# A 64-expert transformer layer: each expert's weights in one transfer, in six joint buffers

## The chip, the core and the metric

The kernel runs on one core of a Trainium2 chip. The core has TensorE (PE) for matrix products, VectorE (DVE), ScalarE (ACT), GpSimd (POOL) and SyncE (SP), which here only issues DMAs, and 16 DMA engines that move data between device memory and SBUF. The engines run side by side and are ordered by semaphores alone. The metric is the device time of one execution in microseconds (us); lower is better.

## The reference, cut to what matters

```python
# x: 4096 tokens of 512; attention with a decaying running sum, then a mixture of 64 experts
x = layernorm(x + attention(x, w_qkv, w_out, decay))

scores = softmax(xf @ gate_w.T)                 # 4096 x 64
topk_w, topk_idx = top_k(scores, 6)
# each expert has up to 128 slots (CAP): buf_tok (64, 128) names tokens, buf_w their weights
gx = xp[buf_tok]                                # 64 x 128 x 512, the gathered rows
g, u = split(einsum("ech,ehi->eci", gx, gate_up_proj))   # gate_up_proj: 64 x 512 x 384
hid = silu(g) * u                               # 64 x 128 x 192
eo = einsum("eci,eih->ech", hid, down_proj) * buf_w      # down_proj: 64 x 192 x 512
routed = zeros.at[buf_tok].add(eo)
shared = (silu(xf @ sg.T) * (xf @ su.T)) @ sd.T          # one shared expert of width 384
x = layernorm(x + routed + shared)
```

All is float32. The kernel reaches that precision by splitting operands into a rounded part (hi, float32r) and a rest (lo), and adding three products.

## The kernel before

The work runs in three stages. First the attention, eight blocks (`NB`) of 512 tokens (`BT`), with the routing of each tile of 128 tokens behind it; it ends at about 460 us. Then the experts, one after another (`NE` = 64), with work units of the shared expert between them. Last the remaining shared units, which take the second normalisation with them.

The order of each engine is written by hand, one function per engine inside `build` (`sync`, `scalar`, `vector`, `gpsimd`, `tensor`). Nothing is scheduled by a tool.

An expert e takes these steps. POOL gathers its 128 rows from `x1_rows` into `xg` (`gather`, 2304 bytes a row, six buffers `NXG`, issued four experts ahead, `AHEAD`). SP loads its gate-up weights (`load_gate_up`, L466, 128 partitions x 6144 bytes) and its down weights (`load_down`, L471, 128 x 3072 bytes). ACT rounds the gate-up weights into `wgu_hi` (`split_expert`, L904), DVE writes the rest `wgu_lo` over the weights in the buffer (L1454). PE turns the rows (`turn_rows`, L1956), multiplies them (L1717), turns the hidden values (L1999), and multiplies them with the down weights (`down`, also L1717, since every product goes through the helper `chain`). ACT scales the output rows by the token weight into `eo` (`scale_rows`, L918), and POOL adds them to the rows in device memory with an indirect DMA (`add_rows`, L1657).

PE's iteration e is: product of expert e, `down(e - 1)`, the shared units of this iteration if it has any (`fills_of`), `turn_rows(e + 2)`, the turn of the hidden values. ACT and DVE convert the weights of e + 2 in iteration e.

There are five gate-up buffers (`NG`) and five down buffers (`ND`). SP's loop for the experts, behind the loads of experts 0 to 4, is:

```python
for e in range(NE):
    if e + NG < NE:
        load_gate_up(e + NG)      # waits until gu_mm >= e + 1: the product of expert e is done
    if e and e - 1 + ND < NE:
        load_down(e - 1 + ND)     # waits until eo_mm >= e: down(e - 1) is done
```

POOL's loop issues `add_rows(e - 2)` and then `gather(e + 4)`. An add waits for its output rows and, since two adds to one of the two sum arrays must not overlap, for the landing of the add two experts before it (`rows_added[e % 2]`). The gather is queued behind it.

The input block of the shared expert (`x1t_stage`, 1 MB) is loaded from ACT's queue (`load_x1t`, L760) once for each eight units.

Three DMA queues appear in the profile: q1 is that of SP, q10 that of ACT, q0 that of POOL.

Of the kernel before, what the change touches and what calls it, by code (L numbers as in the profile page):

```python
# [7 lines left out]
F32 = mybir.dt.float32  # L8
F32R = mybir.dt.float32r
# [6 lines left out]
P = 128  # L16
# [24 lines left out]
def three(a_hi, a_lo, b_hi, b_lo):  # L41

    return [(a_hi, b_hi), (a_hi, b_lo), (a_lo, b_hi)]


def build(nc, x, x_t, w_qkv, w_out, decay_param, gate_t, w_gu, w_down, sg_t, su_t, sd_t, out):
    T, D = x.shape
    E, _, _, GU = w_gu.shape
    I = GU // 2
    SI = sg_t.shape[1]  # L50
    BT = 512
    NB = T // BT
    NJ = BT // P
# [1 line left out]
    KC = D // P  # L55
    SC = SI // P
    IB = I - P
    DH = D // 2
    DN = D + DH
    KS = KC - 0  # L60
    SLOTS = E * CAP
    HW = D // HEADS
    TAIL = 4
    EARLY = NB - TAIL
    SET = 1
    NG, ND, NXG, AHEAD = 5, 5, 6, 4
    STEPS = NB * KC
    UNITS = 2 * SC + NJ // 2

# [9 lines left out]
    both = Map(nc, start, end)  # L79
# [7 lines left out]
    FRING = 8  # L87
    fin_sum, fin_mean, fin_square, fin_rstd, fin_shift = [both.place(f"fin_{s}", [P, FRING])
                                                          for s in ("sum", "mean", "square", "rstd", "shift")]
    wgu_at = [both.at + 4 * i * KC * GU for i in range(2)]  # L90
    wgu_buf = [both.place(f"wgu{i}", [P, KC, GU]) for i in range(2)]
    wdn_buf = [both.place(f"wdn{i}", [P, DN]) for i in range(2)]

    att = Map(nc, both.at, end)
    wqkv_hi = att.place("wqkv_hi", [P, 3 * KC, KC, P], F32R)
# [77 lines left out]
    xs_at = lo_at + KC * chunk  # L173
# [22 lines left out]

    late = Map(nc, projected_end, kept_from)

    wgu_at += [late.at + 4 * i * KC * GU for i in range(NG - 3)]
    wgu_buf += [late.place(f"wgu{i}", [P, KC, GU]) for i in range(2, NG - 1)]  # L200

    wdn_buf += [late.place(f"wdn{i}", [P, DN]) for i in range(2, ND - 1)]
    assert late.at >= projected_end + 8 * 4 * BT

    shared_rows = [late.place(f"shared_rows{b}", [P, NJ, D]) for b in range(EARLY - SET)]
# [2 lines left out]
    xgt_hi = [late.place(f"xgt_hi{i}", [P, KS, P], F32R) for i in range(2)]  # L208
    xgt_lo = [late.place(f"xgt_lo{i}", [P, KS, P], F32R) for i in range(2)]
    eo = [Map(nc, x_at + 2 * half - 4 * D, x_at + 2 * half).place("eo0", [P, D]),  # L210
          Map(nc, xs_at + 4 * BT, xs_at + 8 * BT).place("eo1", [P, D]),
          Map(nc, x_at + 4 * half - 4 * D, x_at + 4 * half).place("eo2", [P, D])]
    silu_e = late.place("silu_e", [P, I])
    hid_e = [late.place(f"hid_e{i}", [P, 2 * P]) for i in range(2)]
    hid_et = [late.place(f"hid_et{i}", [P, P]) for i in range(2)]
    het_hi = [late.place(f"het_hi{i}", [P, P], F32R) for i in range(2)]
    het_lo = [late.place(f"het_lo{i}", [P, P], F32R) for i in range(2)]

# [1 line left out]
    late.end = end  # L220
    wgu_hi = [late.place(f"wgu_hi{i}", [P, KS, GU], F32R) for i in range(2)]
    wdn_mix = [late.place(f"wdn_mix{i}", [P, D], F32R) for i in range(2)]
    xg += [late.place(f"xg{i}", [P, D + E]) for i in range(NXG - 2, NXG)]
    eo.append(late.place("eo3", [P, D]))
    wgu_at.append(late.at)
    wgu_buf.append(late.place(f"wgu{NG - 1}", [P, KC, GU]))
    wdn_buf.append(late.place(f"wdn{ND - 1}", [P, DN]))
    wgu_lo = [Map(nc, at, at + 4 * KC * GU).place(f"wgu_lo{i}", [P, KS, GU], F32R) for i, at in enumerate(wgu_at)]


    fin_map = Map(nc, both.at - 2 * 4 * (KC * GU + DN), both.at)
# [10 lines left out]
    NE, NEO = E, len(eo)  # L242
# [48 lines left out]
    for e in range(NE):  # L291
        n = 0
# [37 lines left out]
    with ExitStack() as ctx:  # L330
# [3 lines left out]
        def sems(name, n):  # L334
            return [sem(f"{name}{i}") for i in range(n)]
# [5 lines left out]
        xg_ps, gu_ps, ht_ps, eo_ps = banks[3], banks[4:6], banks[6], banks[7]  # L341
        hot_ps, last_ps = banks[6], banks[6]

        def rows_bank(i):
# [11 lines left out]

        SCALED, ROUNDED = 1, 2
        TABLE_READ, TABLE_TURNED, TABLE_JOINED = 1, 2, 3
        gu_in, dn_in, xg_in, rows_added = sems("gu_in", NG), sems("dn_in", ND), sems("xg_in", NXG), sems("rows_added", 2)
        zeroed, shared_out, x1t_in = sem("zeroed"), sems("shared_out", SET), sem("x1t_in")  # L360
        fin_in, odd_in, fin_out = sems("fin_in", NFA), sems("odd_in", NFB), sems("fin_out", NFA)

# [14 lines left out]
        xgt_hi_done, wgu_hi_done, silu_e_done, het_hi_done, eo_done = (  # L377
            sem("xgt_hi_done"), sem("wgu_hi_done"), sem("silu_e_done"), sem("het_hi_done"), sem("eo_done"))
# [51 lines left out]
        def _(sp):  # L430
# [29 lines left out]
                    sp.wait_ge(x1_added, i - 1)  # L460
                sp.dma_start(xres[i % 2][:, :], x[i * P:(i + 1) * P, :]).then_inc(xres_in[i % 2], 16)

            def load_gate_up(e):
                if e >= NG:
                    sp.wait_ge(gu_mm, e - NG + 1)
                sp.dma_start(wgu_buf[e % NG][:, :, :], w_gu[e]).then_inc(gu_in[e % NG], 16)  # L466

            def load_down(e):
                if e >= ND:
                    sp.wait_ge(eo_mm, e - ND + 1)  # L470
                sp.dma_start(wdn_buf[e % ND][:, :], w_down[e]).then_inc(dn_in[e % ND], 16)  # L471

            def clear_sums(b):
                dst = acc_dram[1][b * BT:(b + 1) * BT, :].rearrange("(p r) (n w) -> p (r n) w", p=P, w=P)
# [87 lines left out]
            sp.wait_ge(num_done, STEPS)  # L562
            sp.wait_ge(qk_done, STEPS)
            sp.wait_ge(state_done, STEPS)
            for e in range(2, NG - 1):
                load_gate_up(e)
            load_down(2)
            store_turned(LAST - 3)
            store_x1(LAST - 3)
            store_score(LAST - 4)  # L570
            store_x1(LAST - 2)
            sp.wait_ge(heads_mm, NB)
            load_down(3)
            sp.wait_ge(shared_split, 2)
            for e in range(2):
                load_gate_up(e)
            store_turned(LAST - 2)
            store_score(LAST - 3)
            store_score(LAST - 2)
# [3 lines left out]
            load_xres(NB - 1, 3)  # L583
            store_score(LAST - 1)
            sp.wait_ge(shared_split, 2 + SC)
            for e in range(2):
                load_down(e)
            for i in range(LAST, NT):
                store_x1(i)
                store_turned(i)  # L590
# [9 lines left out]
                sp.wait_ge(x1_out[lane], 16 * NT // NJ)  # L600
                sp.wait_ge(acc_out[lane], 16 * NT // NJ)
            sp.wait_ge(table_done, TABLE_JOINED)
            load_gate_up(NG - 1)
            load_down(ND - 1)
            for e in range(NE):
                if e + NG < NE:
                    load_gate_up(e + NG)
                if e and e - 1 + ND < NE:
                    load_down(e - 1 + ND)

            def load_first(m):
                b = block_order[m]
# [38 lines left out]
        def _(act):  # L651
# [246 lines left out]
                act.copy(xgt_hi[e % 2][:, :, :], xg_ps[:, :].rearrange("p (k s) -> p k s", k=KC)).then_inc(xgt_hi_done, 1)  # L898

            def split_expert(e):  # L900
                act.wait_ge(gu_in[e % NG], 16 * (e // NG + 1))
                if e >= 2:
                    act.wait_ge(gu_mm, e - 1)
                act.copy(wgu_hi[e % 2][:, :, :], wgu_buf[e % NG][:, 0:KS, :]).then_inc(wgu_hi_done, 1)  # L904

            def split_down_of(e):
                act.wait_ge(dn_in[e % ND], 16 * (e // ND + 1))
                if e >= 2:
                    act.wait_ge(eo_mm, e - 1)
                w, mix = wdn_buf[e % ND], wdn_mix[e % 2]  # L910
                act.copy(mix[0:IB, 0:DH], w[0:IB, D:DN])
                act.copy(mix[IB:P, DH:D], w[IB:P, D:DN]).then_inc(wdn_hi_done, 1)

# [101 lines left out]
        def _(dve):  # L1015
# [435 lines left out]

            def split_expert(e):
                dve.wait_ge(wgu_hi_done, e + 1)
                dve.tensor_tensor(wgu_lo[e % NG][:, :, :], wgu_buf[e % NG][:, 0:KS, :], wgu_hi[e % 2][:, :, :].bitcast(F32),  # L1454
                                  ALU.subtract).then_inc(wgu_lo_done, 1)

            def split_down_of(e):
                dve.wait_ge(wdn_hi_done, e + 1)
                w, mix = wdn_buf[e % ND], wdn_mix[e % 2]
                dve.tensor_tensor(mix[IB:P, 0:DH], w[0:IB, D:DN], mix[0:IB, 0:DH].bitcast(F32), ALU.subtract)  # L1460
                dve.tensor_tensor(mix[0:IB, DH:D], w[IB:P, D:DN], mix[IB:P, DH:D].bitcast(F32), ALU.subtract).then_inc(wdn_lo_done, 1)

# [251 lines left out]
        def _(pe):  # L1714
            def chain(out_ap, products, first=True, final=True):
                for i, (a, b) in enumerate(products):
                    mm = pe.matmul(out_ap, a, b, start=first and i == 0, stop=final and i == len(products) - 1)  # L1717
                return mm
# [240 lines left out]
            def down(e):  # L1959
                pe.wait_ge(het_lo_done, e + 1)  # L1960
                pe.wait_ge(wdn_lo_done, e + 1)
                if e:
                    pe.wait_ge(eo_done, e)
                products = [(part[e % 2][:, :], wdn_mix[e % 2][:, :]) for part in (het_hi, het_lo)]
                chain(eo_ps[:, :], products, final=False)
                chain(eo_ps[:, :], [(hid_et[e % 2][:, :], wdn_buf[e % ND][:, 0:D])], first=False).then_inc(eo_mm, 1)

            for _ in range(BEFORE_EXPERTS[0]):
                unit()
# [10 lines left out]
            for e in range(NE):  # L1980
                pe.wait_ge(xgt_lo_done, e + 1)
                if e >= 2:
                    pe.wait_ge(hid_e_done, e - 1)
                pe.wait_ge(wgu_lo_done, e + 1)
                products = []
                for k in range(KS):
                    products += three(xgt_hi[e % 2][:, k, :], xgt_lo[e % 2][:, k, :], wgu_hi[e % 2][:, k, :], wgu_lo[e % NG][:, k, :])
                chain(gu_ps[e % 2][:, 0:GU], products).then_inc(gu_mm, 1)
                if e:
                    down(e - 1)  # L1990
                for _ in range(fills_of[e]):
                    unit()
                if e + 2 < NE:
                    turn_rows(e + 2)
                pe.wait_ge(hid_e_done, e + 1)
                if e:
                    pe.wait_ge(het_lo_done, e)
                for h in range(2):
                    mm = pe.transpose(ht_ps[:, h * P:(h + 1) * P], hid_e[e % 2][:, h * P:(h + 1) * P], ident[:, :])  # L1999
                mm.then_inc(ht_mm, 1)  # L2000
# [37 lines left out]
```

## Time and profile before

| | us |
|---|---|
| median of 3 runs | 913.0 |
| the three runs | 909.56, 913.0, 913.59 |
| the profiled execution | 914.21 |
| its span, first to last instruction | 911.6 |
| expert stage, about | 480 to 808 |

The median is the time to compare with. The profiled execution is a single one; its rows sum up to its own time, 2.6 us of which lie outside the span. Busy time of PE is modelled from the starts of its pipelined products. An engine's idle time is shown in brackets, with what ended it behind the arrow.

### The profile page before, as it was taken

Reading aid. Unit: us, or ns where it says so; the run is one execution under the profiler, and the core shown is the slowest. Engines: PE = TensorE matmul, PEld = TensorE weight load, DVE = VectorE, ACT = ScalarE, POOL = GpSimd, SP = SyncE. Lnnn points to the kernel's source line nnn. Section 1 sums busy time; section 2 is a strip of 40 time slices with the busy share of each in tenths; the row PEclk is TensorE's granted clock in tenths of the full one; section 3 lists DMA queues with packets and bytes.
Section 4 is the critical chain, followed back from the end, with each engine's and each line's share of the span. In section 5 each row is a group of like instructions: output and inputs, shape, how many; then the busy total and the mean of one; then the engine's idle time right before and its main releaser. Section 6 shows DMA issues by size and latency. Waiting matters only on the chain. (4 is left out here: it accounts for less than half of the span.)

```text
span 911.6 us, 15597 instructions
## 1 busy us (share of the span) xinstructions
PE 892.3 (98%) x4635; PEld 727.5 (80%) x4635; DVE 718.9 (79%) x1422; ACT 549.0 (60%) x1208; POOL 488.1 (54%) x540
## 2 busy tenths in 40 slices
PE   8999999999999999999999999999999999999997
PEld 7788888888888788777888788888788888877875
DVE  6997887979788897898857788887778887736776
ACT  5532535434353443544558878888778888736785
POOL 2002366565566656577434656766566666533665
PEclk9999999999999999999999999999999999999999
DMA  6343563536263333439567999999999999959963
GB/s 211 97 161 116 145 140 103 133 89 173 74 188 96 123 103 116 144 101 336 181 224 238 333 360 354 357 337 323 348 342 347 336 346 324 298 106 391 378 249 129
DMA packets 111634, 203.95 MB, mean 224 GB/s; under 512 B 18496, under 2 KB 50240, under 8 KB 110528
## 3 DMA queue, kind: packets, MB, share of 16 engines
q1 hardware_dynamic: 91024, 159.87, 51.2%
q0 software_dynamic: 19520, 35.75, 16.3%
q10 hardware_dynamic: 1008, 7.34, 2.1%
q8 instruction: 38, 0.62, 0.3%
q14 instruction: 44, 0.36, 0.1%
HBM read 143.03 MB, written 59.88 MB: 223 GB/s over the span
## 5 line engine op out<-in xcount | busy, mean ns | idle before, releaser
L1612 POOL DMA_INDIRECT slot_table<-tokens,slot_of x162 | 180.3, 1113 | 86.9 <-issue 50.4
L1657 POOL DMA_INDIRECT acc_rows<-eo,table_sb x64 | 137.1, 2142 | 119.8 <-DMA acc_rows<-eo,table_sb 61.8
L1717 PE MATMUL bank<-x_hi,wqkv_hi 128*128 128x512 f32 x384 | 152.1, 396 | 1.6 <-DVE wqkv_lo L1022 1.6
L1717 PE MATMUL bank<-x_hi,wqkv_lo 128*128 128x512 f32 x384 | 150.1, 391 | 0.0
L1717 PE MATMUL bank<-x_lo,wqkv_hi 128*128 128x512 f32 x384 | 150.1, 391 | 0.0
L1454 DVE TENSOR_TENSOR wgu_lo<-wgu,wgu_hi 128x1536 fp32r<-128x1536 f32 x64 | 112.1, 1752 | 2.6 <-ACT wgu_hi L904 1.9
L904 ACT CAST wgu_hi<-wgu 128x1536 fp32r<-128x1536 f32 x64 | 94.2, 1473 | 1.6 <-issue 0.4
L1646 POOL DMA_INDIRECT xg<-x_rows,table_sb x64 | 73.4, 1147 | 36.3 <-issue 19.0
L1717 PE MATMUL bank<-wgu_hi,xgt_hi 128*128 128x384 f32 x256 | 91.9, 359 | 0.0
L674 ACT ACTIVATE e<-bank 128x512 f32<-128x512 f32 x64 | 38.0, 594 | 81.4 <-PE bank L1717 81.4
L1717 PEld LDWEIGHTS bank<-x_hi,wqkv_hi 128*128 128x128 f32 x384 | 72.2, 188 | 17.5 <-DVE wqkv_lo L1022 1.8
L1717 PE MATMUL bank<-wgu_lo,xgt_hi 128*128 128x384 f32 x256 | 86.1, 336 | 0.0
L1717 PE MATMUL bank<-wgu_hi,xgt_lo 128*128 128x384 f32 x256 | 86.0, 336 | 0.0
L1717 PEld LDWEIGHTS bank<-x_hi,wqkv_lo 128*128 128x128 f32 x384 | 72.0, 188 | 15.5
L1717 PEld LDWEIGHTS bank<-x_lo,wqkv_hi 128*128 128x128 f32 x384 | 72.2, 188 | 15.1
L1596 POOL TENSOR_SCALAR rstd<-mv 128x1 f32<-128x1 f32 x32 | 9.8, 307 | 123.1 <-DVE mv L1049 121.9
L1717 PE MATMUL bank<-wdn,hid_et 128*128 128x512 f32 x128 | 65.3, 591 | 0.0
L1956 PEld LDWEIGHTS bank<-ident,xg 128*128 128x128 f32 x256 | 30.4, 141 | 33.8 <-issue 25.2
L1467 DVE TENSOR_TENSOR het_lo<-bank,het_hi 128x128 fp32r<-128x128 f32 x64 | 18.6, 291 | 45.3 <-ACT het_hi L957 45.0
L1717 PE MATMUL bank<-wout_hi,att_hi 128*128 128x512 f32 x128 | 52.3, 408 | 1.1 <-issue 0.6
L1717 PE MATMUL bank<-wout_lo,att_hi 128*128 128x512 f32 x128 | 50.2, 393 | 0.0
L1717 PE MATMUL bank<-wout_hi,att_lo 128*128 128x512 f32 x128 | 50.2, 392 | 0.0
(198 smaller groups left out, 2300.0 us busy)
## 6 DMA issues: line engine op xcount, KB each, us to landing
wgu<-w_gu SPq DMA_DIRECT2D x64, 768.0 KB, 7.3
wdn<-w_down SPq DMA_DIRECT2D x64, 384.0 KB, 8.0
xres<-x SPq DMA_DIRECT2D x32, 256.0 KB, 3.4
x_turned<-x1t SPq DMA_DIRECT2D x32, 256.0 KB, 2.9
x_rows<-x SPq DMA_DIRECT2D x32, 256.0 KB, 3.1
acc_rows<-x SPq DMA_DIRECT2D x32, 256.0 KB, 2.8
fin<-acc_rows SPq DMA_DIRECT2D x8, 1024.0 KB, 11.9
odd<-acc_rows SPq DMA_DIRECT2D x8, 1024.0 KB, 13.9
```

The lines of the kernel that those rows point to most:

```text
L674: act.activation(e_sb[q][:, :], ps[:, :], ACT.Exp)
L904: act.copy(wgu_hi[e % 2][:, :, :], wgu_buf[e % NG][:, 0:KS, :]).then_inc(wgu_hi_done, 1)
L1454: dve.tensor_tensor(wgu_lo[e % NG][:, :, :], wgu_buf[e % NG][:, 0:KS, :], wgu_hi[e % 2][:, :, :].bitcast(F32), ALU.subtract).then_inc(wgu_ ...
L1467: dve.tensor_tensor(het_lo[e % 2][:, :], ht_ps[:, P:2 * P], het_hi[e % 2][:, :].bitcast(F32), ALU.subtract).then_inc(het_lo_done, 1)
L1596: pool.tensor_scalar(rstd[i][:, :], mv[i][:, 1:2], EPS_NORM, None, ALU.add).then_inc(norm_done, 1)
L1612: pool.indirect_dma_start(table_dram, bass.IndirectOffsetOnAxis(slot_of[:, i, k:k + 1], 0), tokens[:, i:i + 1], None, bounds_check=SLOTS - ...
L1646: pool.indirect_dma_start(xg[e % NXG][:, :], None, x1_dram, bass.IndirectOffsetOnAxis(table_sb[:, e:e + 1], 0), bounds_check=T - 1, oob_is ...
L1657: pool.indirect_dma_start(acc_dram[e % 2], bass.IndirectOffsetOnAxis(table_sb[:, e:e + 1], 0), eo[eo_slot[e]][:, :], None, bounds_check=T ...
L1717: mm = pe.matmul(out_ap, a, b, start=first and i == 0, stop=final and i == len(products) - 1)
L1956: mm = pe.transpose(xg_ps[:, k * P:(k + 1) * P], xg[e % NXG][:, k * P:(k + 1) * P], ident[:, :])
```

## The change

The host places an expert's down weights behind its gate-up weights, so that both are one row of 9216 bytes for each partition (`w_expert`). One DMA (`load_expert`) fills one of six joint buffers (`NW` = 6), with one semaphore (`we_in`). The buffer is free when `down` of its former expert is done (`eo_mm`); gate-up and down weights are views of it. The first six experts are loaded ahead: 2, 3, 0 and 1 during the last attention block, 4 and 5 when the routing table is ready. To make room, `silu_e` and `hid_et` lie where the `tanh_s` tile of shared block 0 stood.

```diff
-    NG, ND, NXG, AHEAD = 5, 5, 6, 4
+    NW, NXG, AHEAD = 6, 6, 4
...
-    silu_e = late.place("silu_e", [P, I])
+    small = Map(nc, xs_at, xs_at + 4 * BT)
+    silu_e = small.place("silu_e", [P, I])
     hid_e = [late.place(f"hid_e{i}", [P, 2 * P]) for i in range(2)]
-    hid_et = [late.place(f"hid_et{i}", [P, P]) for i in range(2)]
+    hid_et = [small.place(f"hid_et{i}", [P, P]) for i in range(2)]
...
+    we_at += [late.at + 4 * i * WE for i in range(NW - 4)]
+    we_buf += [late.place(f"we{i}", [P, WE]) for i in range(4, NW)]
+    wgu_buf = [we[:, 0:KC * GU].rearrange("p (k n) -> p k n", k=KC) for we in we_buf]
+    wdn_buf = [we[:, KC * GU:WE] for we in we_buf]
...
-            def load_gate_up(e):
-                if e >= NG:
-                    sp.wait_ge(gu_mm, e - NG + 1)
-                sp.dma_start(wgu_buf[e % NG][:, :, :], w_gu[e]).then_inc(gu_in[e % NG], 16)
-
-            def load_down(e):
-                if e >= ND:
-                    sp.wait_ge(eo_mm, e - ND + 1)
-                sp.dma_start(wdn_buf[e % ND][:, :], w_down[e]).then_inc(dn_in[e % ND], 16)
+            def load_expert(e):
+                if e >= NW:
+                    sp.wait_ge(eo_mm, e - NW + 1)
+                sp.dma_start(we_buf[e % NW][:, :], w_expert[e]).then_inc(we_in[e % NW], 16)
...
-            for e in range(2, NG - 1):
-                load_gate_up(e)
-            load_down(2)
+            load_expert(2)
...
             sp.wait_ge(heads_mm, NB)
-            load_down(3)
+            load_expert(3)
             sp.wait_ge(shared_split, 2)
-            for e in range(2):
-                load_gate_up(e)
+            load_expert(0)
...
             sp.wait_ge(shared_split, 2 + SC)
-            for e in range(2):
-                load_down(e)
+            load_expert(1)
...
-            load_gate_up(NG - 1)
-            load_down(ND - 1)
-            for e in range(NE):
-                if e + NG < NE:
-                    load_gate_up(e + NG)
-                if e and e - 1 + ND < NE:
-                    load_down(e - 1 + ND)
+            for e in range(4, NE):
+                load_expert(e)
...
             def split_expert(e):
-                act.wait_ge(gu_in[e % NG], 16 * (e // NG + 1))
+                act.wait_ge(we_in[e % NW], 16 * (e // NW + 1))
...
             def split_down_of(e):
-                act.wait_ge(dn_in[e % ND], 16 * (e // ND + 1))
+                act.wait_ge(we_in[e % NW], 16 * (e // NW + 1))
```

SP's order moves; the other engines keep theirs. These rows are of SP, at the start of the expert stage, before the change (the number in a name tells the buffer; `gu_mm` and `eo_mm` count products and down products done):

```order
234 L471 DMA wdn_211<-w_down 128x768
235 L466 DMA wgu_70<-w_gu 128x1536 [waits gu_mm]
236 L466 DMA wgu_71<-w_gu 128x1536 [waits gu_mm]
237 L471 DMA wdn_72<-w_down 128x768 [waits eo_mm]
238 L466 DMA wgu_176<-w_gu 128x1536 [waits gu_mm]
239 L471 DMA wdn_73<-w_down 128x768 [waits eo_mm]
```

The same place of SP with the change, from the load of expert 3's successor, expert 4 (buffer 206):

```order
228 L475 DMA acc_rows<-shared_rows_176 128x4x512 [waits rows_copied]
229 L466 DMA we_206<-w_expert 128x2304 [waits x1_out2,acc_out1,acc_out2,x1_out1,x1_out3,acc_out0,acc_out3,x1_out0,table_done,x1t_out1,x1t_out0]
230 L466 DMA we_207<-w_expert 128x2304
231 L466 DMA we_70<-w_expert 128x2304 [waits eo_mm]
232 L466 DMA we_71<-w_expert 128x2304 [waits eo_mm]
```

Expert 5's weights (row 230) now follow those of expert 4 without a wait, and every later expert is one load that waits for a down product.

During the last attention block SP's queue had this before the change:

```order
192 L466 DMA wgu_176<-w_gu 128x1536 [waits state_done,qk_done,num_done]
193 L466 DMA wgu_177<-w_gu 128x1536
194 L471 DMA wdn_178<-w_down 128x768
195 L484 DMA x_turned<-x1t_143 512x1x128 [waits x1t_done]
...
201 L471 DMA wdn_179<-w_down 128x768 [waits heads_mm]
202 L466 DMA wgu_70<-w_gu 128x1536 [waits shared_split]
203 L466 DMA wgu_71<-w_gu 128x1536
...
213 L471 DMA wdn_72<-w_down 128x768 [waits shared_split]
214 L471 DMA wdn_73<-w_down 128x768
```

And with the change:

```order
192 L466 DMA we_174<-w_expert 128x2304 [waits state_done,qk_done,num_done]
193 L479 DMA x_turned<-x1t_141 512x1x128 [waits x1t_done]
...
199 L466 DMA we_175<-w_expert 128x2304 [waits heads_mm]
200 L466 DMA we_70<-w_expert 128x2304 [waits shared_split]
...
210 L466 DMA we_71<-w_expert 128x2304 [waits shared_split]
```

Eight loads became four, at the places of the later half of each pair; expert 1 (`we_71`) moved behind eight stores and loads, to where its down half was.

## Rows read from the trace of the kernel before

In a row of waits stand the waiting engine and line, what ended the wait, total us, times and the longest. A row of a timeline has start and duration in us, engine, line, operation and how many. A row of a DMA queue has packets, MB and the share of 16 engines' time; a row of an issue has how many, KB, and the middle time from issue to landing in us.

**Rows 1.** The page: busy us and share of PE; DMA share in 40 slices.

```profile
PE 892.3 (98%) x4635; PEld 727.5 (80%) x4635; DVE 718.9 (79%) x1422; ACT 549.0 (60%) x1208; POOL 488.1 (54%) x540
DMA  6343563536263333439567999999999999959963
```

**Rows 2.** Busy us by stretch: PE, PEld, DVE, ACT, POOL; granted clock, DMA share, GB/s.

```profile
480.00:808.00 328.00, 323.04 (x1653) 267.17 (x1652) 257.79 (x466) 263.94 (x540) 200.14 (x121) 0.99 0.99 324
656.80:660.00 3.20, 3.20 (x13) 3.20 (x14) 1.22 (x2) 1.61 (x5) 0.32 (x1) 0.50 1.06 362
```

**Rows 3.** Waits in 486 to 808 us.

```profile
POOL acc_rows L1657 <- DMA acc_rows<-eo,table_sb: 61.8, 30, 3.6
...
PEld bank L1956 <- DMA xg<-x_rows,table_sb: 5.6, 4, 2.9
...
PE bank L1956 <- DMA xg<-x_rows,table_sb: 2.5, 2, 2.0
```

**Rows 4.** Timeline of PE: the longest wait for gathered rows.

```profile
656.73 1.12 PE L1956 MATMUL bank<-ident,xg 128*128 128x128 f32 x4 [2.04 <-DMA xg<-x_rows,table_sb]
```

**Rows 5.** Timelines of POOL and PE, and between them this gather's time to landing.

```profile
548.37 1.06 POOL L1646 DMA_INDIRECT xg<-x_rows,table_sb  x1 [0.31 <-issue]
...
xg<-x_rows,table_sb POOLq DMA_INDIRECT x1, 7.7
...
556.79 0.60 PE L1956 MATMUL bank<-ident,xg 128*128 128x128 f32 x4
```

**Rows 6.** Timeline of SP's issues in 600 to 606 us, and gate-up landings.

```profile
601.04 0.33 SPq L466 DMA_DIRECT2D wgu<-w_gu  x1
602.37 0.33 SPq L471 DMA_DIRECT2D wdn<-w_down  x1
605.31 0.33 SPq L466 DMA_DIRECT2D wgu<-w_gu  x1
...
DMA to landing us min/median/max: 5.0/7.5/11.4
```

**Rows 7.** DMA queues and issues of POOL in 486 to 800 us.

```profile
q1 hardware_dynamic: 16835, 68.74, 57.5%
q0 software_dynamic: 13280, 32.84, 41.7%
q10 hardware_dynamic: 432, 3.15, 2.4%
...
acc_rows<-eo,table_sb POOLq DMA_INDIRECT x61, 9.1
xg<-x_rows,table_sb POOLq DMA_INDIRECT x58, 7.8
```

**Rows 8.** DMA queues in 651 to 654 us, while x1t_stage is loaded.

```profile
q10 hardware_dynamic: 87, 0.71, 56.0%
q0 software_dynamic: 87, 0.28, 25.9%
q1 hardware_dynamic: 68, 0.22, 18.9%
```

**Rows 9.** DMA queues in 657 to 663 us.

```profile
q1 hardware_dynamic: 335, 1.35, 56.9%
q0 software_dynamic: 305, 0.82, 48.9%
```

**Rows 10.** The first expert's gather: POOL's issue, its landing, PE's transposes.

```profile
462.51 1.06 POOL L1646 DMA_INDIRECT xg<-x_rows,table_sb  x1 [16.97 <-DVE table_sb L1183]
...
xg<-x_rows,table_sb POOLq DMA_INDIRECT x1, 8.2
...
471.89 0.60 PE L1956 MATMUL bank<-ident,xg 128*128 128x128 f32 x4
```

More of the change, by code:

```diff
@@ L43, in three, with build @@
     return [(a_hi, b_hi), (a_hi, b_lo), (a_lo, b_hi)]
-def build(nc, x, x_t, w_qkv, w_out, decay_param, gate_t, w_gu, w_down, sg_t, su_t, sd_t, out):
+def build(nc, x, x_t, w_qkv, w_out, decay_param, gate_t, w_expert, sg_t, su_t, sd_t, out):
     T, D = x.shape
-    E, _, _, GU = w_gu.shape
+    E, SI = w_expert.shape[0], sg_t.shape[1]
+    GU = (w_expert.shape[2] - D - D // 2) // (D // P)
     I = GU // 2
-    SI = sg_t.shape[1]
     BT = 512
@@ L59, in build @@
     DN = D + DH
+    WE = KC * GU + DN
     KS = KC - 0
@@ L89, in build @@
                                                           for s in ("sum", "mean", "square", "rstd", "shift")]
-    wgu_at = [both.at + 4 * i * KC * GU for i in range(2)]
-    wgu_buf = [both.place(f"wgu{i}", [P, KC, GU]) for i in range(2)]
-    wdn_buf = [both.place(f"wdn{i}", [P, DN]) for i in range(2)]
+    we_at = [both.at + 4 * i * WE for i in range(2)]
+    we_buf = [both.place(f"we{i}", [P, WE]) for i in range(2)]
     att = Map(nc, both.at, end)
@@ L197, in build @@
     late = Map(nc, projected_end, kept_from)
-    wgu_at += [late.at + 4 * i * KC * GU for i in range(NG - 3)]
-    wgu_buf += [late.place(f"wgu{i}", [P, KC, GU]) for i in range(2, NG - 1)]
-    wdn_buf += [late.place(f"wdn{i}", [P, DN]) for i in range(2, ND - 1)]
+    we_at += [late.at + 4 * i * WE for i in range(2)]
+    we_buf += [late.place(f"we{i}", [P, WE]) for i in range(2, 4)]
     assert late.at >= projected_end + 8 * 4 * BT
@@ L224, in build @@
     eo.append(late.place("eo3", [P, D]))
[L225 to L228, printed above, removed]
+    we_at += [late.at + 4 * i * WE for i in range(NW - 4)]
+    we_buf += [late.place(f"we{i}", [P, WE]) for i in range(4, NW)]
+    wgu_buf = [we[:, 0:KC * GU].rearrange("p (k n) -> p k n", k=KC) for we in we_buf]
+    wdn_buf = [we[:, KC * GU:WE] for we in we_buf]
+    wgu_lo = [Map(nc, at, at + 4 * KC * GU).place(f"wgu_lo{i}", [P, KS, GU], F32R) for i, at in enumerate(we_at)]
     fin_map = Map(nc, both.at - 2 * 4 * (KC * GU + DN), both.at)
@@ L358, in build @@
         TABLE_READ, TABLE_TURNED, TABLE_JOINED = 1, 2, 3
-        gu_in, dn_in, xg_in, rows_added = sems("gu_in", NG), sems("dn_in", ND), sems("xg_in", NXG), sems("rows_added", 2)
+        we_in, xg_in, rows_added = sems("we_in", NW), sems("xg_in", NXG), sems("rows_added", 2)
         zeroed, shared_out, x1t_in = sem("zeroed"), sems("shared_out", SET), sem("x1t_in")
@@ L900, in split_expert @@
             def split_expert(e):
-                act.wait_ge(gu_in[e % NG], 16 * (e // NG + 1))
+                act.wait_ge(we_in[e % NW], 16 * (e // NW + 1))
                 if e >= 2:
                     act.wait_ge(gu_mm, e - 1)
-                act.copy(wgu_hi[e % 2][:, :, :], wgu_buf[e % NG][:, 0:KS, :]).then_inc(wgu_hi_done, 1)
+                act.copy(wgu_hi[e % 2][:, :, :], wgu_buf[e % NW][:, 0:KS, :]).then_inc(wgu_hi_done, 1)
             def split_down_of(e):
-                act.wait_ge(dn_in[e % ND], 16 * (e // ND + 1))
+                act.wait_ge(we_in[e % NW], 16 * (e // NW + 1))
                 if e >= 2:
                     act.wait_ge(eo_mm, e - 1)
-                w, mix = wdn_buf[e % ND], wdn_mix[e % 2]
+                w, mix = wdn_buf[e % NW], wdn_mix[e % 2]
                 act.copy(mix[0:IB, 0:DH], w[0:IB, D:DN])
@@ L1453, in split_expert @@
                 dve.wait_ge(wgu_hi_done, e + 1)
-                dve.tensor_tensor(wgu_lo[e % NG][:, :, :], wgu_buf[e % NG][:, 0:KS, :], wgu_hi[e % 2][:, :, :].bitcast(F32),
+                dve.tensor_tensor(wgu_lo[e % NW][:, :, :], wgu_buf[e % NW][:, 0:KS, :], wgu_hi[e % 2][:, :, :].bitcast(F32),
                                   ALU.subtract).then_inc(wgu_lo_done, 1)
@@ L1458, in split_down_of @@
                 dve.wait_ge(wdn_hi_done, e + 1)
-                w, mix = wdn_buf[e % ND], wdn_mix[e % 2]
+                w, mix = wdn_buf[e % NW], wdn_mix[e % 2]
                 dve.tensor_tensor(mix[IB:P, 0:DH], w[0:IB, D:DN], mix[0:IB, 0:DH].bitcast(F32), ALU.subtract)
@@ L1965, in down @@
                 chain(eo_ps[:, :], products, final=False)
-                chain(eo_ps[:, :], [(hid_et[e % 2][:, :], wdn_buf[e % ND][:, 0:D])], first=False).then_inc(eo_mm, 1)
+                chain(eo_ps[:, :], [(hid_et[e % 2][:, :], wdn_buf[e % NW][:, 0:D])], first=False).then_inc(eo_mm, 1)
             for _ in range(BEFORE_EXPERTS[0]):
@@ L1986, in _ @@
                 for k in range(KS):
-                    products += three(xgt_hi[e % 2][:, k, :], xgt_lo[e % 2][:, k, :], wgu_hi[e % 2][:, k, :], wgu_lo[e % NG][:, k, :])
+                    products += three(xgt_hi[e % 2][:, k, :], xgt_lo[e % 2][:, k, :], wgu_hi[e % 2][:, k, :], wgu_lo[e % NW][:, k, :])
                 chain(gu_ps[e % 2][:, 0:GU], products).then_inc(gu_mm, 1)
@@ L2026 @@
         "decay_param": decay, "gate_t": a["L0_ffn_gate_w"].T,
-        "w_gu": gu, "w_down": down,
+        "w_expert": np.concatenate([gu.reshape(experts, P, -1), down], axis=2),
         "sg_t": a["L0_ffn_shared_gate_w"].T, "su_t": a["L0_ffn_shared_up_w"].T, "sd_t": a["L0_ffn_shared_down_w"].T,
```

## Prediction

> **What bounds the kernel now.** I read the page first, then the idle times by what ended them, then the DMA queues of the expert stage. The page says that PE is busy for 98% of the span [rows 1], so the end is set by TensorE and only its gaps can be won. In the expert stage, 480 to 808 us, it is idle for 328.0 - 323.0 = 5.0 us, while the 16 DMA engines are occupied 0.99 of the time [rows 2]. So two things are full at once: PE does about 328 / 64 = 5.13 us of work per expert, and the DMA engines carry about as much as they can in that time. The expert stage contains everything that the change touches.
>
> The reader should next look at who makes PE wait there. PE waits for no weights. It waits for the gathered token rows (xg): 2.5 us on the matmuls in 2 cases, 5.6 us on the weight loads in 4 [rows 3]. The longest case is at 656.73 us: 2.04 us idle before the transposes of xg [rows 4]. Right behind it the granted clock is 0.50, which is the 1.2 GHz level, for the 3.2 us of 656.8 to 660 [rows 2], where PE does half as much: another 1.6 us. One late gather thus cost about 3.6 us. The gathers are thin elsewhere too. The one issued at 548.37 took 7.7 us and landed at 556.07, and its transposes started at 556.79, a margin of 0.7 us [rows 5]. POOL, which issues them, itself waits 61.8 us in 30 cases for an earlier add of output rows to land before it may issue the next add, and each gather stands behind such an add in its queue [rows 3].
>
> The weights have room. A gate-up load goes out when the product of expert e-5 ends and is converted during iteration e-2, three iterations later. The shortest iterations last 605.31 - 601.04 = 4.27 us, so the lead is at least 12.8 us, against landings of 7.5 us in the middle and 11.4 us at worst [rows 6].
>
> **The change part by part.**
>
> *Issues.* 128 weight transfers become 64. SP only waits in the loop and nothing but the next weight load is queued behind it, so the 64 issues less are worth nothing on any path.
>
> *Placement of the load.* Both orders show it: the joint load waits for eo_mm where gate-up waited for gu_mm. It is issued where the down load stands now, 602.37 - 601.04 = 1.33 us after the gate-up load [rows 6]. For gate-up that is 1.33 us later, for down one iteration earlier. The lead becomes 12.8 - 1.3 = 11.5 us. The joint landing I take as 7.5 us plus 384 KB at the stage's 324 GB/s [rows 2], 1.2 us, so 8.7 us: 2.8 us of margin, and zero on PE. If the worst landing (11.4 + 1.2 = 12.6) met the shortest three iterations, PE would lose 1.1 us; that is the bound upward, and there is none below zero, since PE never waited for weights.
>
> *DMA work.* In 486 to 800 us the weight queue q1 holds 57.5% of 314 us, the gather-and-add queue q0 41.7% [rows 7]; the 58 gathers issued there count the experts. Per expert and DMA engine q1 has 3.11 us in 16835 / 16 / 58 = 18.1 packets, 0.172 us each; q0 has 2.26 us in 14.3 packets, 0.158 us each. A row of gate-up (6 KB) and one of down (3 KB) become one packet of 9 KB; with the completion entries q1 has 9 packets per expert instead of 18. What that saves lies between nothing and the price per byte of the 8 KB packets of q10: 56.0% of 16 x 3 us for 0.71 MB, 37.9 us per MB, against 56.9% of 16 x 6 us for 1.35 MB, 40.5 us per MB, for q1 now [rows 8, 9]. That is at most 6%, 0.2 us of 3.11 per expert; 9 KB is nearest to 8 KB, so I take 0.2. It is DMA time, not PE time: it only shows where a gather was late.
>
> *Turns between the queues.* This is the term that decides. In 657 to 663 us, both queues full, q1 sends 335 packets and q0 305 [rows 9]; in 651 to 654 us, with a third queue loading the shared block's input, q10, q0 and q1 send 87, 87 and 68 packets, but 0.71, 0.28 and 0.22 MB [rows 8]. The engines share by packets, not by bytes. The Trainium skill, page DMA: Bandwidth & Descriptors, section Queues, rings and completion order, says that an engine goes round the queues that have work, packet by packet; the trace agrees by those counts. So a q0 packet today waits for a q1 packet of 0.172 us; the 14.3 packets of one expert need 14.3 x (0.158 + 0.172) = 4.72 us when q1 always has work. Afterwards they meet all nine weight packets, 2.26 + (3.11 - 0.2) = 5.17 us. q0 gets through later by 0.45 us per expert. Since the gather stands behind an add that waits for an earlier add, it can be hit twice: 0.9 us, bounds 0 (if the turns fall between bursts) and 1.5. The weights land sooner in exchange, where nobody waits.
>
> At 0.9 us the two stalls that PE has deepen by 1.8 us together, and margins like the 0.7 us of [rows 5] turn into 0.2 us each; I allow three: 0.6 us. Sum: +2.4 us.
>
> *Start of the stage.* Expert 5's load now goes out right behind expert 4's, together with the first gathers, instead of after the first product. The first gather is issued at 462.51 and lands 8.2 us later; its transposes start at 471.89, 1.2 us of margin [rows 10]. Its four packets per engine would each wait for 0.32 us instead of 0.17, 0.6 us in all, so the margin covers it: zero. If the gather had to wait for all of the extra 2.9 us of weights, 1.7 us would be lost. Expert 1 is loaded where its down half stood, among the last blocks of the attention and well ahead of the gathers: zero. The six buffers and the moved small ones wait for nothing new, because the tanh tile is last used in shared block 0, which ends before the experts: zero.
>
> **Sum.** The profiled execution took 914.2 us, 1.2 above the median of 913.0. 914.2 + 2.4 = 916.6, less 1.2: about **915.5 us**.
>
> **The rivals.**
>
> *Add chain (slower).* If q0 takes longer per expert than PE, POOL falls behind and every gather is late. The point is 5.13 us per expert. By the above q0 needs 5.17 us, and the three block loads of q10 add 2.4% of 314 us, 0.13 us per expert [rows 7]: 5.30. Over 58 experts 0.17 x 58 = 10 us, less the 2 us of margin that gathers have on the way: +8 us, 921 us. For it: POOL already waits for adds in 30 of 61 cases. Against it: the experts that carry a shared unit take longer, and q0 catches up there, and the shares of [rows 8, 9] add up to over 100%, so packets overlap a little.
>
> *Relief (faster).* Less DMA work and one burst instead of two leave the engines a pause, the gather at 656.73 lands in time, and 2.0 + 1.6 us go, with the 0.4 us of the other stall: 914.2 - 4.1 - 1.2 = 909 us. More is not to be had, since PE waits for nothing else of the change. For it: the fastest of the three runs, 909.56 us, lies just there, as if one run had had no such stall. Against it: q0's turn gets worse while the total falls by under 4%. The rules for kernel authors on the same page of the Trainium skill ask for DMAs of 1 MiB and more, and by its fit (2.0 us plus bytes at 436 GB/s) two loads of 3.8 and 2.9 us would become one of 4.7, an estimate of 2.0 us per expert; these loads overlap with others, so no PE time follows, and it speaks for this rival alone.
>
> *No effect.* The hardware cuts a 9 KB row into packets of the old size. Then turns and prices stay, and only the 1.33 us later issue is left: 913 us.
>
> **How the numbers follow.** Chances: the forecast 0.40 (913 to 917.5), the add chain 0.30, relief 0.22, no effect 0.08. About 0.5%, 4.6 us, is what a measurement of this kernel can tell from no change. Slower by more: the add chain without its mild end, 0.28, and 0.04 from the forecast's upper bound. Faster by more would need less than 908.4 us, 0.10 of the relief case. The range 909 to 922 takes in the relief value and the add chain's 921; outside lie its worse forms.
>
> **What would show it.** Packets of 9 KB in q1, nine per engine and expert. The middle landing of gathers above 7.8 us and of adds above 9.1 us, the weights' landing little above 7.5 us; PE's wait for xg above 2.5 us, always in front of the transposes. More of POOL's wait on adds than 61.8 us would point to the chain. Gathers landing sooner than now would prove the turn term wrong, and PE waiting for the weight conversion would prove the margin wrong.

## The result, and the profile after

The changed kernel takes 936.82 us at the median (934.69 to 937.7), against 913.05 us before: ratio 1.0259, 95% interval 1.0238 to 1.0279. It is 24 us slower where 2.5 us were forecast, and lies outside the range. The profiled execution took 936.49 us with a span of 934.7 us, so the rows below account for 23 us of span. A few executions of the later sets ran far slower than the rest (984 to 2593 us) and are left out of every ratio.

The stretches of the expert stage answer to [rows 2]; the columns are those of that group.

```profile
480.00:830.00 350.00, 325.43 (x1653) 265.96 (x1651) 257.96 (x466) 265.75 (x542) 189.16 (x120) 1.00 0.96 301
809.10:812.50 3.40, 3.40 (x12) 3.40 (x12) 2.56 (x3) 1.61 (x5) 2.15 (x2) 0.51 0.84 202
```

The stage now lasts until about 830 us instead of 808. PE's idle time in it is 350.0 - 325.4 = 24.6 us, where it was 5.0 us, and PE is busy 2.4 us longer for the same 1653 matmuls: 22 of the 23 us of span are here. DVE and ACT are busy as long as before, and the DMA engines move less per second (301 GB/s against 324). There is one clock drop again, to 0.51 in 809.1 to 812.5 us. As before, it stands right behind one of the longest waits for gathered rows, the one that ends at 808.22.

Who made PE wait is told by the waits of 480 to 830 us, against [rows 3]:

```profile
POOL acc_rows L1643 <- DMA acc_rows<-eo,table_sb: 88.3, 36, 4.5
...
PEld bank L1942 <- DMA xg<-x_rows,table_sb: 42.4, 28, 4.2
...
PE bank L1942 <- DMA xg<-x_rows,table_sb: 23.1, 20, 3.4
```

The gathered rows it is, 23.1 us in 20 cases instead of 2.5 us in 2. No row of waits names the weights. The longest cases in PE's timeline, against [rows 4]:

```profile
523.99 0.66 PE L1942 MATMUL bank<-ident,xg 128*128 128x128 f32 x4 [1.65 <-DMA xg<-x_rows,table_sb]
...
663.93 0.55 PE L1942 MATMUL bank<-ident,xg 128*128 128x128 f32 x3 [3.36 <-DMA xg<-x_rows,table_sb]
...
808.22 0.66 PE L1942 MATMUL bank<-ident,xg 128*128 128x128 f32 x4 [3.00 <-DMA xg<-x_rows,table_sb]
```

The DMA queues and issues of 486 to 820 us, against [rows 7]:

```profile
q1 hardware_dynamic: 8352, 68.42, 55.9%
q0 software_dynamic: 13244, 32.80, 40.9%
q10 hardware_dynamic: 432, 3.15, 2.3%
...
we<-w_expert SPq DMA_DIRECT2D x58, 1152.0 KB, 8.8
...
acc_rows<-eo,table_sb POOLq DMA_INDIRECT x60, 10.2
xg<-x_rows,table_sb POOLq DMA_INDIRECT x58, 9.6
```

q1 has half the packets for the same bytes: 8352 / 16 / 58 = 9 per engine and expert. A gather takes 9.6 us to land at the median instead of 7.8, an add 10.2 instead of 9.1. Both queues in 640 to 655 us, around the longest wait, first before the change and then with it:

```profile
q1 hardware_dynamic: 645, 2.67, 45.7%
q0 software_dynamic: 660, 1.66, 42.7%
...
q1 hardware_dynamic: 394, 3.32, 62.7%
q0 software_dynamic: 532, 1.32, 36.2%
```

Over the 16 engines q0 gets 532 / 15 = 35 packets per us here, where it got 660 / 15 = 44, with q10 at work beside it. This is a bad stretch and not the rule: in 664 to 670 us it gets 282 / 6 = 47, and over the whole window it falls only from 13280 / 314 = 42 to 13244 / 334 = 40. Six of these 15 us, 645 to 651, show the turns at their clearest. q1 sends 166 packets and q0 142, nearly one for one as in [rows 9], and that is 24 per us for q0. One gather issued in this stretch takes 14.7 us to land.

### The profile page after: what moved, and what is told of

It is laid out like the page before. It is cut to its first block and busy times, and to the rows that moved or that the text cites. A ratio compares the mean times of both kernels' runs of the same rounds, so it can differ in the third digit from the quotient of the medians.

```text
span 934.7 us, 15533 instructions
## 1 busy us (share of the span) xinstructions
PE 895.7 (96%) x4635; PEld 727.4 (78%) x4635; DVE 719.0 (77%) x1422; ACT 549.9 (59%) x1208; POOL 476.9 (51%) x540
## 5 line engine op out<-in xcount | busy, mean ns | idle before, releaser
L1643 POOL DMA_INDIRECT acc_rows<-eo,table_sb x64 | 125.0, 1953 | 152.9 <-DMA acc_rows<-eo,table_sb 88.3
L1440 DVE TENSOR_TENSOR wgu_lo<-we,wgu_hi 128x1536 fp32r<-128x1536 f32 x64 | 112.0, 1752 | 2.6 <-ACT wgu_hi L890 1.9
L890 ACT CAST wgu_hi<-we 128x1536 fp32r<-128x1536 f32 x64 | 94.2, 1473 | 1.6 <-issue 0.4
L1703 PE MATMUL bank<-we,hid_et 128*128 128x512 f32 x128 | 65.3, 592 | 0.0
L1942 PE MATMUL bank<-ident,xg 128*128 128x128 f32 x256 | 39.8, 278 | 23.6 <-DMA xg<-x_rows,table_sb 23.1
## 6 DMA issues: line engine op xcount, KB each, us to landing
odd<-acc_rows SPq DMA_DIRECT2D x8, 1024.0 KB, 13.9
```

The costliest lines, as they stand in the source:

```text
L890: act.copy(wgu_hi[e % 2][:, :, :], wgu_buf[e % NW][:, 0:KS, :]).then_inc(wgu_hi_done, 1)
L1440: dve.tensor_tensor(wgu_lo[e % NW][:, :, :], wgu_buf[e % NW][:, 0:KS, :], wgu_hi[e % 2][:, :, :].bitcast(F32), ALU.subtract).then_inc(wgu_ ...
L1643: pool.indirect_dma_start(acc_dram[e % 2], bass.IndirectOffsetOnAxis(table_sb[:, e:e + 1], 0), eo[eo_slot[e]][:, :], None, bounds_check=T ...
L1942: mm = pe.transpose(xg_ps[:, k * P:(k + 1) * P], xg[e % NXG][:, k * P:(k + 1) * P], ident[:, :])
```

## The experiments

Two theories stood against each other. **Turns:** the DMA engines serve the queues packet by packet, so larger weight packets make every packet of a gather or an add wait longer. **Burst:** what harms is that 1.15 MB are issued in one piece, later, and on top of the gather. A third, **chain**, puts the loss down to POOL's order, in which the gather stands behind an add that waits for an earlier add. All ratios below are to the kernel before, run on the same chip. They are not the quotients of the two medians and differ from them by up to 0.2%. The runs came in three sets on three chips, and each trace is of a single execution.

### The joint load with 3 KB packets

Only the layout in device memory changes; the DMA, its place and its wait stay.

```diff
-sp.dma_start(we_buf[e % NW][:, :], w_expert[e])
+sp.dma_start(we_buf[e % NW][:, :].rearrange("p (c n) -> p c n", c=3), w_expert[e].rearrange("c p n -> p c n"))
```

> The changed kernel with one edit: in device memory an expert's weights lie in three pieces of 3072 bytes for each partition, so the joint load stays one DMA at the same place with the same wait, but moves 3 KB packets instead of 9 KB ones. Theory turns (DMA engines serve the queues packet by packet, so a gather or add packet waits for a whole weight packet): a gather or add packet waits for 0.12 us of weights instead of 0.36, gathers land in 7.8 us or less at the median, PE's wait for gathered rows falls from 23 us to under 3, 909 to 914 us. Theory burst (the load of 1.15 MB in one piece, 1.3 us later and on top of the gather, is what delays it): nothing moves, 935 to 938 us, gathers at 9.6 us.

Measured: 913.84 us, ratio 1.0029 (1.0008 to 1.0049). Its waits in 486 to 830 us, then its issues in 486 to 800 us:

```profile
POOL acc_rows L1643 <- DMA acc_rows<-eo,table_sb: 43.5, 22, 3.6
...
PE bank L1942 <- DMA xg<-x_rows,table_sb: 2.7, 2, 1.5
ACT wgu_hi L890 <- DMA we<-w_expert: 0.9, 2, 0.6
```

```profile
we<-w_expert SPq DMA_DIRECT2D x57, 1152.0 KB, 11.6
...
xg<-x_rows,table_sb POOLq DMA_INDIRECT x58, 7.6
```

The wait for gathered rows falls from 23.1 to 2.7 us, and the loss falls from 2.6% to 0.3%. (This trace is of the fastest of the ten executions, 911.41 us, so the wait at the median may be somewhat longer.) The weights pay, 11.6 us instead of 8.8. That is what turns said and what burst excludes: the same bytes are issued at the same moment.

### The joint buffers with two loads

```diff
-sp.dma_start(we_buf[e % NW][:, :], w_expert[e]).then_inc(we_in[e % NW], 16)
+sp.dma_start(we_buf[e % NW][:, 0:KC * GU], w_expert[e][:, 0:KC * GU]).then_inc(we_in[e % NW], 16)
+sp.dma_start(we_buf[e % NW][:, KC * GU:WE], w_expert[e][:, KC * GU:WE]).then_inc(we_in[e % NW], 16)
```

The two waits for `we_in` count to 32 instead of 16.

> The changed kernel with the joint load issued as two DMAs, gate-up (6 KB packets) and down (3 KB packets) directly behind each other, behind the same wait for the down product, into the same joint buffers. Theory turns: the packets of before are back, so 912 to 917 us, PE's wait for gathered rows 2 to 6 us; what is left over 913 is the price of the later issue. Theory burst: the same bytes still arrive at the same moment, 934 to 938 us.

Measured: 916.19 us, ratio 1.0022 (1.0002 to 1.0042). PE waits 5.6 us for gathered rows:

```profile
PE bank L1943 <- DMA xg<-x_rows,table_sb: 5.6, 3, 3.3
```

With the packets of before, nearly all of the loss is gone, by a second edit that leaves the moment of issue alone. It also leaves the weights in device memory where the changed kernel has them, so their layout there is not the cause either. What stays above the kernel before is 0.2%, 0.4% at the upper end of the interval. That is the most that the later issue can have cost here.

### The gather ahead of the add

```diff
 for e in range(NE):
-    if e >= 2:
-        add_rows(e - 2)
     if e + AHEAD < NE:
         gather(e + AHEAD)
+    if e >= 2:
+        add_rows(e - 2)
```

> The changed kernel, with POOL issuing the gather of expert e + 4 ahead of the add of expert e - 2 instead of behind it; packets and loads stay as changed. Theory chain (a gather is late mostly because it stands behind an add that waits for an earlier add to land): the gather goes out 1 to 4 us sooner in the 36 cases in which POOL waits, and nearly all of the loss goes, 913 to 917 us. Theory direct (the gather's own packets wait in the DMA engines): gathers still take 9.6 us from issue to landing, and half or more of the loss stays, 922 to 932 us.

Measured: 932.36 us, ratio 1.0207 (1.0186 to 1.0228). The waits in 480 to 830 us and the issues in 486 to 800 us:

```profile
POOL acc_rows L1643 <- DMA acc_rows<-eo,table_sb: 96.9, 40, 6.3
...
PE bank L1942 <- DMA xg<-x_rows,table_sb: 15.4, 11, 3.4
```

```profile
xg<-x_rows,table_sb POOLq DMA_INDIRECT x57, 8.9
acc_rows<-eo,table_sb POOLq DMA_INDIRECT x56, 10.1
```

Only some 4.5 us of the 24 come back, though PE waits 7.7 us less for gathered rows. Three stretches of the stage now run at a granted clock of 0.50 (561.4 to 564.8, 660.4 to 663.8 and 766.2 to 769.6 us), where the changed kernel had one. A gather takes 8.9 us to land instead of 9.6, so 0.7 of its 1.8 us may have come from the add issued just ahead of it; the same order in a form with 3 KB packets, below, shows no such gain.

So the add directly in front of a gather is the smaller part. The run does not take the chain away: each gather still stands behind the add of the expert before, and POOL waits even longer for adds to land, 96.9 us in 40 cases. The time is also just above the 922 to 932 us expected of the direct theory. What the wait between adds costs, no run shows.

### The kernel before with 3 KB gate-up packets

```diff
-sp.dma_start(wgu_buf[e % NG][:, :, :], w_gu[e])
+sp.dma_start(wgu_buf[e % NG][:, :, :].rearrange("p (c k) n -> p c (k n)", c=2), w_gu[e].rearrange("c p n -> p c n"))
```

> The kernel before with one edit: the gate-up weights lie in two pieces of 3072 bytes for each partition, so that all weight packets are 3 KB; loads, buffers and order are untouched. Theory turns: a gather packet waits for 0.12 us of weights instead of 0.17 on average, gathers land under 7.8 us at the median, PE's 2.5 us of waits for gathered rows and the clock drop behind the longest go, 909 to 911 us; PE has no more to win. Theory burst: nothing moves, 912 to 914 us.

Measured: 910.05 us, ratio 0.9976 (0.9963 to 0.9989), faster than both kernels. Its waits for DMAs in 486 to 830 us, and its issues in 486 to 800 us:

```profile
POOL acc_rows L1657 <- DMA acc_rows<-eo,table_sb: 41.7, 23, 3.4
PEld bank L1956 <- DMA xg<-x_rows,table_sb: 3.6, 4, 0.9
```

```profile
wgu<-w_gu SPq DMA_DIRECT2D x57, 768.0 KB, 10.4
...
xg<-x_rows,table_sb POOLq DMA_INDIRECT x58, 7.3
```

PE's own waits for gathered rows are gone and so is the clock drop, the gate-up weights land 2.9 us later than in [rows 6], and nobody waits for them. So the same lever works from the other side, in a kernel whose buffers, loads and order nobody touched.

### The joint load with 4.5 KB packets

The edit is that of the 3 KB form with two pieces instead of three.

> The changed kernel with the weights of an expert in two pieces of 4608 bytes for each partition: one DMA, the same place and wait, 4.5 KB packets. Theory turns, by size: a gather or add packet waits for 0.18 us of weights, about the mean of the kernel before (6 KB and 3 KB packets), so 913 to 918 us and gathers at 7.8 to 8.2 us. Rival edge (only packets over some size are handled worse): then it equals the 3 KB form, 912 to 914.5 us, and the loss lies between 4.5 and 9 KB alone. Rival count (what matters is that the number of weight rows fell): between the 3 KB and 9 KB forms, nearer to 9 KB, 920 to 930 us.

Measured: 917.29 us, ratio 1.0035 (1.0013 to 1.0057).

```profile
PE bank L1942 <- DMA xg<-x_rows,table_sb: 7.4, 3, 4.6
...
xg<-x_rows,table_sb POOLq DMA_INDIRECT x58, 8.4
```

By time alone it can't be told from the 3 KB form, since the intervals overlap. The gathers tell them apart: 8.4 us at the median against 7.6, and 9.6 with 9 KB. So for the gathers there is no edge that only 9 KB packets cross; they land later with each larger size. The time does not follow in proportion: 0.35% is lost at 4.5 KB and 2.6% at 9 KB. The gathers land a little later than expected (7.8 to 8.2 us), and later than beside the mixed packets before. The count of rows as a cause falls too, it wanted 920 to 930 us.

### The kernel before with 1.5 KB gate-up packets

> The kernel before with the gate-up weights in four pieces of 1536 bytes for each partition; down stays at 3 KB. Theory turns: gathers and adds get through sooner still (gather under 7.3 us), but the weights now give way: they land at 12 us or more against a lead of 12.8 us, so ScalarE and then PE wait for weights in places, 911 to 918 us. If packets this small cost nothing and the weights keep up, 909 to 910.5 us.

Measured: 910.82 us, ratio 0.9979 (0.9968 to 0.9991), no different from the 3 KB form. Its issues in 486 to 800 us, and what ACT waited:

```profile
wgu<-w_gu SPq DMA_DIRECT2D x57, 768.0 KB, 13.0
...
xg<-x_rows,table_sb POOLq DMA_INDIRECT x58, 6.9
```

```profile
ACT wgu_hi L904 <- DMA wgu<-w_gu: 0.3, 1, 0.3
```

The gathers win another 0.4 us that nobody needs, and the weights come to the edge of their lead (12.8 us by [rows 6]). I expected a loss there, 911 to 918 us; one wait of 0.3 us is all that came of it. A likely reason, which no run tests, is that most iterations are longer than the shortest: the turns of rows of 62 experts start between 481.7 and 798.1 us in the trace of before, 316.4 / 61 = 5.19 us each, so the lead is mostly about 15 us.

### The shared block's input in 2 KB packets

```diff
-x1t_dram = nc.dram_tensor("x1_turned", (NB, P, KC, BT), F32, kind="Internal").ap()
+x1t_dram = nc.dram_tensor("x1_turned", (NB, KC, P, BT), F32, kind="Internal").ap().rearrange("b k p t -> b p k t")
```

> The kernel before with 3 KB gate-up packets and the shared block's input in 2 KB packets instead of 8 KB ones (the turned rows lie chunk by chunk in device memory). Theory turns: the gathers that run beside this load, the slowest of the 3 KB kernel at 10.0, 9.4 and 9.8 us, land at 9 us or less, and their margins of 0.2 us grow; PE has at most 1 us left to win, 909 to 910.5 us, with fewer runs near 912. If the amount of data and not the packet is what slows them, those gathers stay at 9.4 to 10 us and the time at 910.1 us with the same spread.

Measured: 910.22 us, ratio 0.9968 (0.9955 to 0.9981). The gathers' times to landing, first of the kernel before with 3 KB packets, then with this edit added:

```profile
DMA to landing us min/median/max: 5.4/7.3/10.0
```

```profile
DMA to landing us min/median/max: 5.2/7.4/8.7
```

The worst gather falls from 10.0 to 8.7 us while the middle stays, and the input itself takes 13.9 us instead of 9.3, the middle landing of before in 486 to 800 us. This fits turns in a third queue, by one trace on either side: the same bytes in smaller packets hold up the gathers less. The time can't be told from 910.05 us.

### The gather ahead of the add, with 3 KB packets

> The kernel before with 3 KB gate-up packets and POOL's gather of expert e + 4 ahead of the add of expert e - 2. Theory: gathers go out 1 us or more sooner where POOL waits for an add, which removes what waits for rows are left; 909 to 910.5 us. Rival: an add is now behind a gather, adds end later, and the last ones hold up the final stage by about 1 us: 910.5 to 912 us.

Measured: 910.05 us, ratio 0.996 (0.9947 to 0.9973). In its stage PE waits for no row and no weight; POOL's wait for adds is 25.4 us:

```profile
POOL acc_rows L1657 <- DMA acc_rows<-eo,table_sb: 25.4, 16, 3.2
POOL xg L1646 <- DMA acc_rows<-eo,table_sb: 8.5, 7, 2.2
```

The time is that of the 3 KB form; the later adds cost nothing that could be seen. Gathers land in 7.8 us at the median instead of the 7.3 of that form, adds in 7.9 instead of 8.9.

### The joint load with 1.5 KB packets

> The changed kernel with an expert's weights in six pieces of 1536 bytes for each partition, still one DMA behind the down product's wait. Theory turns: gathers land in 7.0 us and PE waits under 1 us for them, but the weights get the short end: their landing of 11.6 us in the 3 KB form grows to 14 us and more, over the lead of 11.5 us that the joint wait leaves, so the waits move to ScalarE's conversion of the weights, 3 us and more in all, and the time is 914 to 922 us, above the 3 KB form. If small packets only help, it is 909 to 912 us.

Measured: 915.12 us, ratio 1.0023 (1.0012 to 1.0034).

```profile
ACT wgu_hi L890 <- DMA we<-w_expert: 9.8, 8, 2.3
...
PE bank L1942 <- DMA xg<-x_rows,table_sb: 1.0, 1, 1.0
```

The weights land in 13.4 us at the median, over the lead of 11.5 us, and the waits move to ACT's conversion, as expected. They land a little sooner than the 14 us expected. The time is not clearly above the 3 KB form, whose interval covers it. So none of the four sizes tried brings the joint load down to the separate ones: small packets make the weights late, large ones the gathers. That its shorter lead (by 1.3 us) is what leaves no size between is argued, not tested.

### All three edits

> The kernel before with the three edits that helped or did no harm: 3 KB gate-up packets, 2 KB packets for the shared block's input, the gather ahead of the add. Theory: PE no longer waits for rows or weights in the expert stage, so they don't add up: 909 to 910.5 us, as each of the two pairs. If they add up, 907 to 908.5 us.

Measured: 909.95 us, ratio 0.9964 (0.9951 to 0.9977). They don't add up: in this trace PE waits for no row and no weight in the stage, and it is busy for 327.26 of the 330 us from 480 to 810 us, as in the 3 KB form without the other two edits. The rest of the time is PE's own work.

## Why the prediction was wrong

**What bounds the kernel, and where it is thin: right.** Of the DMAs PE waited for gathered rows alone, and nearly all of the loss came there.

**Placement and weights: right.** The joint load lands in 8.8 us at the median (8.7 forecast), and nobody waits for it. The 3 KB and 1.5 KB forms show the 11.5 us of lead from the other side: at a landing of 11.6 us ACT's first waits appear (0.9 us), at 13.4 us they are 9.8 us.

**Start of the stage: right.** The second load beside the first gathers cost PE nothing: the first gather landed in 8.5 us instead of 8.2, and PE was busy for all of the 18.0 us from 462 to 480.

**DMA work: wrong.** I took 0.2 us per expert off q1 for the larger packets. Measured, q1 holds 55.9% of 334 us for 58 experts, 3.22 us each, against 3.11 before. Per MB that is 43.7 us against 42.0. There was no relief. All queues together even took more: 99.1% of 334 us is 331 us, against 101.6% of 314 us, 319 us, for nearly the same bytes. It would be tempting to put the loss down to these 12 us of dearer transfers. The joint load with 1.5 KB packets speaks against it, in 486 to 800 us:

```profile
q1 hardware_dynamic: 45472, 68.42, 62.2%
q0 software_dynamic: 13192, 32.69, 40.5%
q10 hardware_dynamic: 432, 3.15, 2.4%
```

That is 105.1% of 314 us, 330 us of transfers, in a kernel that loses 0.2%. (Shares above 100% mean that packets overlap.) So the engines' total alone does not set the time. Why the 9 KB packets take the engines more time, no run shows.

**Turns: the mechanism right, its size wrong.** The trade by packets was read rightly from [rows 8, 9], and the five packetings of the joint load (9, 6 and 3, 4.5, 3, 1.5 KB) bear it out. The failing step is the one that turned the lateness into PE time: "I allow three" margins of 0.2 us and two deeper stalls, +2.4 us. That treats the delay as a one-time shift of each gather by 0.9 us. The gathers came 1.8 us later from issue to landing at the median, twice that, and the add waits in front of them grew from 61.8 to 88.3 us. Larger margins than 0.7 us were then used up, and PE waited in 20 cases instead of about five. The trace of before could have warned: from issue, landing and transposes of the gathers of experts 4 to 63, 4 have a margin under 1 us, but 16 under 2 us and 32 under 3 us.

**The rival add chain came nearest, and it was priced too low,** 921 us. It compared 5.30 us of q0's and the block loads' time per expert with PE's 5.13. Without the relief that did not come its own sum reads 2.26 + 3.11 + 0.13 = 5.50 us, 0.37 us over PE, 21 us over 58 experts; PE's extra idle time is 19.6 us. The agreement is no proof. The same three terms add up to 5.50 us in the kernel before, which ran at 5.13 us (5.19 by the starts of its turns): there packets overlapped, and it was the weights that waited in line, with room to do so. What the larger packets changed is who waits.

Whether q0 is held up by its packets' turns alone, or by the wait between adds on top, stays open. An estimate says that the chain was near its own limit: the add two experts on waits for this one to land, so an add has two rounds, 2 x 5.13 = 10.3 us. Adds landed in 9.1 us at the median before, and in 10.2 us with the change. With the gather ahead of the add most of the loss stayed, but that order keeps the wait between adds, so it does not decide this.

**Why 0.30 was too little for it.** I had 4.72 us before and 5.17 us after against 5.13 us of PE, a queue that goes from 92% full to over 100%. By these numbers a step across that line was as likely as a shift of a margin, and deserved to be the forecast.

The estimate of 2.0 us per expert given under relief does not fit these loads: the Trainium skill, page DMA: Bandwidth & Descriptors, section Anatomy of one DMA, gives that fit for a DMA issued from GpSimd, and the weights are SP's. No term of the sum used it.

## What to carry to other kernels

In this kernel, whose DMA engines are full, the size of a packet is a priority: the queue with the larger packets gets the bytes, and the one with small packets waits. Look which stream has room and which has none, and cut the rows of the one with room; here 3 KB instead of 6 KB for weights that had 5 us to spare gave 0.2% (0.1 to 0.4), and the joint load with 9 KB took 2.6%. When a queue's time per round, waits for other queues included, comes near the bound's time per round, compare these rates first. If they leave room, list the margins of all rounds, and not only the thinnest.

## What the runs showed of the hardware that was not expected

Larger packets were no cheaper per byte under load: q1's time per MB in the expert stage was 43.7 us with 9 KB packets, 42.0 with 6 and 3 KB in separate loads and 42.8 in the joint buffers, and 42.7 with 3 KB alone (58.2% of 16 x 314 us for 68.42 MB). Only at 1.5 KB does it rise clearly, to 45.7 (62.2% of the same). And the landings followed the size in both directions: gathers landed at the median in 9.6, 8.4, 7.6 and 6.9 us beside joint loads of 9, 4.5, 3 and 1.5 KB packets, while those loads took 8.8, 9.7, 11.6 and 13.4 us.
